# The last tile's closing layer norm and residual: a shorter merge, the inverse root on GpSimd, and scale and residual fused on VectorE

## The reference

```python
x = x + LN(attention(LN(x)))     # 16 heads of 8, projections with bias
x = x + LN(ffn(LN(x)))           # 32 experts, top 6 of 4 of 8 groups, squared relu, and a shared expert
```

## Time and profile before

| | |
|---|---|
| three runs | 541.24 us median (538.66, 541.24, 541.57) |
| the profiled execution | 542.95 us, of which 540.9 us are the span from the first to the last instruction |
| granted TensorE clock | 0.98 on average |
| busy | PE 90%, DVE 74%, ACT 66%, POOL 32% of the span |
| last matmul group of the feed-forward part | ends at about 531.0 us of the span |
| last tile's closing norm, from the copy at 530.99 to the end | 9.9 us |

### The profile page before, as it was taken

One profiled execution on the slowest core, in us unless ns is written; L12 is line 12 of the kernel. 1 busy time (PEld: TensorE's weight loads), 2 busy tenths in 40 slices (PEclk: granted clock), 3 DMA queues, 4 the chain that ended last, 5 costly groups with the idle time before them and its releaser, 6 DMA issues.

```text
span 540.9 us, 10853 instructions
## 1 busy us (share of the span) xinstructions
PE 484.6 (90%) x3376; PEld 270.5 (50%) x3376; DVE 398.8 (74%) x1072; ACT 359.0 (66%) x708; POOL 170.8 (32%) x500
## 2 busy tenths in 40 slices
PE   2457997989999999998899999999999999999993
PEld 1212443444444444444345665666656665666661
DVE  4678786879999989898725859587776859485453
ACT  2424786758888988888685566757756666755442
POOL 5054231323544435320002223515152533302020
PEclk9999999989999999999699999999999999999998
DMA  6334356333333333331014343535263544535321
GB/s 186 108 118 144 97 173 195 122 117 116 106 110 98 114 109 115 115 114 38 3 60 141 117 162 118 193 103 196 87 179 115 180 157 138 196 100 197 138 78 39
DMA packets 52456, 67.47 MB, mean 125 GB/s; under 512 B 5168, under 2 KB 36784, under 8 KB 52144
## 3 DMA queue, kind: packets, MB, share of 16 engines
q1 hardware_dynamic: 52400, 66.78, 39.2%
HBM read 51.17 MB, written 15.20 MB: 123 GB/s over the span
## 4 chain that ended last, share of the span: by engine, by line
PE 70%; DVE 7%; ACT 7%; SPq 5%; issue 5%; POOL 3%; DMA 2%; ACTq 0%; POOLq 0%; DVEq 0%
PE pY L1278 12%; PE pS L1278 12%; PE pO L1199 8%; PE pS L1264 6%; PE pS L1266 6%; PE pS L1265 6%; PE pS L1143 6%; PE pS L1149 3%; DVE mneg L859 3%; ACT probs L643 2%; SPq L387 2%; SPq L375 2%; PE pX L1128 2%; DMA k_scratch<-k_parts 2%; PE pX L1131 1%
## 5 line engine op out<-in xcount | busy, mean ns | idle before, releaser
L859 DVE TENSOR_REDUCE mneg<-pS 128x2 f32<-128x512 f32 x256 | 164.2, 686 | 31.8 <-PE pS L1143 31.0
L643 ACT ACTIVATE probs<-pS 128x512 f32<-128x512 f32 x256 | 143.9, 595 | 31.7 <-PE pS L1149 30.3
L718 ACT ACTIVATE h_ring<-r 128x512 f32<-128x512 f32 x144 | 90.4, 629 | 88.9 <-DVE r L1013 68.3
L1013 DVE SCALAR_TENSOR_TENSOR r<-pS,c_ring 128x512 f32<-128x512 f32 x128 | 87.6, 689 | 45.6 <-PE pS L1266 44.2
L1143 PE MATMUL pS<-kp,qp 48*128 48x256 bf16 x512 | 88.8, 295 | 24.9 <-DVE mneg L859 9.9
L1264 PE MATMUL pS<-qp,up_hi 128*128 128x512 f32 x144 | 103.5, 719 | 0.0
L1149 PE MATMUL pS<-qp,kp 51*128 51x256 bf16 x512 | 89.1, 287 | 0.8 <-ACT probs L643 0.5
L1199 PE MATMUL pO<-probs,vv 128*32 128x256 f32 x1024 | 76.6, 408 | 0.4 <-ACT oT_sb L594 0.4
L1278 PE MATMUL pS<-h_ring,down_sb 128*128 128x512 f32 x144 | 73.8, 594 | 0.0
L1278 PE MATMUL pY<-h_ring,down_sb 128*128 128x512 f32 x144 | 73.4, 595 | 0.0
L1143 PEld LDWEIGHTS pS<-kp,qp 48*128 48x128 bf16 x512 | 34.9, 97 | 75.3 <-DVE mneg L859 41.7
(11 more groups left out here) (178 smaller groups left out, 682.3 us busy)
## 6 DMA issues: line engine op xcount, KB each, us to landing
c_ring<-c_scratch SPq DMA_DIRECT2D x64, 512.0 KB, 3.9
qp<-q_scratch SPq DMA_DIRECT2D x64, 96.0 KB
kp<-k_scratch SPq DMA_DIRECT2D x64, 96.0 KB
q_scratch<-q_parts SPq DMA_DIRECT2D x16, 192.0 KB, 2.3
k_scratch<-k_parts SPq DMA_DIRECT2D x16, 192.0 KB, 2.4
q_scratch<-q_parts SPq DMA_DIRECT2D x16, 128.0 KB, 2.2
k_scratch<-k_parts SPq DMA_DIRECT2D x16, 128.0 KB, 2.2
out_x<-ot SPq DMA_DIRECT2D x7, 256.0 KB, 4.5
```

Source lines behind the costliest of these rows:

```text
L643: nc.scalar.activation(probs[j][:, hh], pS2[n % S2_RING][:, :, :], ACT.Exp, scale=SCALE).then_inc(exp_done, 1)
L718: nc.scalar.activation(h_sb[n % HRING], r_sb[n % URING][:, :], ACT.Square).then_inc(sq_done, 1)
L859: nc.vector.tensor_reduce(mneg[u % 2][:, :, hh, k], pS1[n % S1_RING][:, :].rearrange("p (a s) -> p a s", a=TH), AX.X, ALU.max, negate=True ...
L1013: nc.vector.scalar_tensor_tensor(out=r_sb[n % URING][:, :], in0=pU[n % URING], scalar=0.0, in1=c_ring[group % CRING][:, at], op0=ALU.max, ...
```

## The change

Only the closing norm of tile 7 is changed.

- **Merge.** 0.25·d·d is now one instruction (`scalar_tensor_tensor`) in place of two (L324 and L327), and the −0.5·m of L325 is no longer an instruction. The order is d, m, v, then v/128 + eps, 0.25·d·d, v + that.
- **Root.** DVE signals `var4_done` after the variance. POOL, at the end of its stream, waits for it and writes `rs4` = variance to the power −0.5, then signals `root4_done`. The Newton rounds, `half` and `nm4` of this tile are gone.
- **Mean.** DVE subtracts the mean from all four pieces in one instruction, `fn` = −0.5·m + `pN`, 128 × 512, with m (128 × 4) broadcast.
- **Scale and residual.** DVE does `ot` = `fn`·rs4 + `xbig` in one instruction of 128 × 128 for each of the four pieces, with `rs4` as a scalar for each partition. Every second one raises `ot_last`. ACT's four `norm_f` pieces of this tile, and DVE's two adds, are gone.
- SP's two stores and their waits are the same.

```diff
@@ gpsimd, after the loop over the tiles
+            pool.wait_ge(var4_done, 1)
+            nc.gpsimd.tensor_tensor(rs4[:, :], work4[0][:, :], power[:, 0:C4], ALU.pow).then_inc(root4_done, 1)
@@ scalar, norm_f
-                if i == NTILE - 1:
-                    ins.then_inc(fn_last, 1)
-                elif c == C4 - 1:
+                if c == C4 - 1:
                     ins.then_inc(fn_done, 1)
@@ scalar, the end
             keep_fT(NTILE - 1)
-            for c in range(C4):
-                norm_f(NTILE - 1, c)
@@ vector, the end
             stats_f(NTILE - 1)
             dve.wait_ge(f_stats, NTILE)
-            norm_chain(nc.vector, dve.wait_ge, Link(dve, ln4_last, 0), stats4[:, :, :], [w[:, :] for w in work4],
-                       rs4[:, :], nm4[:, :], (fn_done, NTILE - 1), fused=True).then_inc(ln4_done, 1)
-            for half in range(2):
-                dve.wait_ge(fn_last, C4 // 2 * (half + 1))
-                if half == 0:
-                    dve.wait_ge(stored[(NTILE - 1) % 2], 16 * (NTILE // 2 - 1))
-                cs = slice(C4 // 2 * half, C4 // 2 * (half + 1))
-                nc.vector.tensor_tensor(ot[(NTILE - 1) % 2][:, cs], fn[:, cs],
-                                        xbig[:, NT - C4 + cs.start:NT - C4 + cs.stop], ALU.add).then_inc(ot_last, 1)
+            v, t, m, d, half = [w[:, :] for w in work4]
+            even, odd = stats4[:, :, 0:3], stats4[:, :, 3:6]
+            link = Link(dve, ln4_last, 0)
+            nc.vector.tensor_tensor(d, even[:, :, 1], odd[:, :, 1], ALU.subtract)
+            nc.vector.tensor_tensor(m, even[:, :, 1], odd[:, :, 1], ALU.add)
+            link(nc.vector.tensor_tensor(v, even[:, :, 2], odd[:, :, 2], ALU.add))
+            nc.vector.tensor_scalar(v, v, 1.0 / D, EPS, ALU.mult, ALU.add)
+            link(nc.vector.scalar_tensor_tensor(out=d, in0=d, scalar=0.25, in1=d, op0=ALU.mult, op1=ALU.mult))
+            nc.vector.tensor_tensor(v, v, d, ALU.add).then_inc(var4_done, 1)
+
+            dve.wait_ge(fn_done, NTILE - 1)
+            dve.wait_ge(ot_done, NTILE - 1)
+            link(nc.vector.scalar_tensor_tensor(out=fn[:, :, :], in0=m.unsqueeze(2).to_broadcast((P, C4, D)), scalar=-0.5,
+                                                in1=pN[:, :].rearrange("p (c d) -> p c d", c=C4),
+                                                op0=ALU.mult, op1=ALU.add))
+            dve.wait_ge(stored[(NTILE - 1) % 2], 16 * (NTILE // 2 - 1))
+            dve.wait_ge(root4_done, 1)
+            for c in range(C4):
+                ins = nc.vector.scalar_tensor_tensor(out=ot[(NTILE - 1) % 2][:, c], in0=fn[:, c], scalar=rs4[:, c:c + 1],
+                                                     in1=xbig[:, NT - C4 + c], op0=ALU.mult, op1=ALU.add)
+                if c % 2:
+                    ins.then_inc(ot_last, 1)
```

More of the change, by code:

```diff
@@ L291, in block_kernel @@
         fn_done = sem("fn_done")
-        fn_last = sem("fn_last")
+        var4_done, root4_done = sem("var4_done"), sem("root4_done")
         ln4_last = sem("ln4_last")
```

## The result

Over 13 runs the changed kernel has a median of 538.91 us (536.74 to 541.86), the kernel before, in 13 runs (three of them those known before the prediction), 542.5 (538.66 to 544.81). The ratio is 0.9949, with a 95% interval of 0.9928 to 0.9970: faster, by 0.3% to 0.7%. The two medians by themselves lie 3.6 us apart, 0.66%, which this interval also holds. The forecast was 539.0 and 2.2 us, 0.41%, within it too. The median of the ratio lies just past the 0.5% that I had called the limit of what can be told; its interval holds both sides of it.

The account below looks back on a forecast made before the run. Matmuls bound the whole span, a serial chain the tail. Merge 0.27, root by POOL 1.12 and last pass 0.85 make 2.24; 2.2 off the median 541.24 gives 539.0 us, range 536.5 to 540.3.

Parts of the forecast that it names:

- Merge: Tile 7's closing statistics: variance ready at 534.05 in place of 534.32, 0.27 us saved by the new order.
- Power: Root on POOL: starts 0.08 behind DVE's variance and takes 1.04, from 534.13 to 535.17.
- Subtraction: DVE's mean subtraction: 0.69, broadcast at no cost, hidden under the power with 0.55 to spare.
- Back to DVE: Hand-over from POOL's power to DVE's first piece: 0.04, so DVE goes on at 535.21.
- Pieces: Four scale-and-residual instructions on DVE: steps of 0.26, duration 0.34, 1.12 in all; bounds 0.89 and 1.36.
- Stores: SP's two issues at L462: 0.52 apart, before 0.69; 2.3 from the second issue to the end.
- Sum: Whole tail: second store begins at 536.35 in place of 538.58, 2.23 us saved.
- shared read path: Rival: the subtraction holds up POOL's power, all behind it 0.53 later, gain 1.7, 539.5; chance 0.07.
- The power was not long: Rival, slower than before: a power of 3.3 us takes all the gain, 4.20 ends at 542.2; chance 0.02.
- Tile 6's store: Rival, no effect: this store, landing at about 532.4, ends the span if it takes 6 us more; chance 0.01.
- A measured ratio past 0.5%: Rival: the gain shows as over 0.5%, with cheaper pieces and power 2.5 us, 0.46%, 538.7; chance 0.2.
- A sign that was wrong: Stated sign: the prediction is wrong if the time before 533 us has moved, which nothing in the change explains.

Follow-up runs that it names:

- e4: Changed kernel with the root made by Newton rounds on DVE again, ahead of the subtraction; merge start to last issue 4.76 us, against 3.19.
- e3: Changed kernel with the subtraction reading `fT_sb` (SBUF) in place of `pN` (PSUM); power 1.40 in place of 1.02, merge start to last issue 3.585 us.
- e1: Changed kernel with the root's wait written first of the three ahead of the first piece; merge start to last issue 3.08 us, against 3.19.
- e2: Changed kernel with pieces multiplying by constant 1.0 in place of rs4; pieces 0.90 in place of 1.14, merge start to last issue 2.96 us.
- e5: Changed kernel with the last pass undone (nm4, four ACT pieces, two adds), short merge and POOL's root kept; merge start to last issue 4.10 us.
- e10: e2 with the second store issued from ACT's queue; merge start to last issue 2.94 us, to the end of the span 5.28.
- e9: e8 with three stores (pieces 0 and 1 SP, 2 ACT, 3 SP); tail 5.14 us, median 539.98, ratio 0.9959 to the kernel before.
- e6: Changed kernel with the power in two instructions of 2 columns and the root's wait first; merge start to last issue 2.905 us.
- e8: Changed kernel with powers of 3 and 1 columns, subtraction written into PSUM, root's wait first; merge start to last issue 2.905 us, tail 5.22.

## Why the prediction was right

- **Merge.** Forecast v + d ending 0.79 behind the merge's start, measured 531.50 − 530.72 = 0.78. The fused 0.25·d·d takes 0.16, as its neighbours.
- **Power.** DVE to POOL 0.08, as forecast; 1.02, where 1.04 was taken (the value of L529 in rows 4, not of L333 in rows 3).
- **Subtraction.** 0.69, under the power, over 0.49 before it ends: 531.42 + 0.69 = 532.11 against 532.60. Its broadcast costs nothing: 0.69 as in L1013. e4 shows what the cover is worth, 0.72, and e3 what it would cost to read both tensors from SBUF, 0.4. The forecast speaks of seven linked DVE steps that the power replaces; nine Newton instructions follow each other by links (e4 has them again, in 2.04). The sum did not use the count.
- **Back to DVE.** The one term that was off: 0.14 in place of 0.04. I had taken the 0.04 from a piece with one late wait, and passed over that the new piece has three waits ahead of it, and that the late one was written last. Everything else was within 0.02. e1 gives the 0.10 back by their order alone.
- **Pieces.** Forecast 1.12, measured 1.14. e2 confirms the split, a step of 0.20 and 0.06 for the scalar. Rows 7, from which the 0.06 came, compare instructions that also differ in where they read and in the type they write, so that it came out exactly is partly luck. The pieces do overlap. The rule quoted from the Trainium skill (VectorE: DVE Perf Modes, The DRAIN you can't avoid), by which they would take 1.36, was quoted without the exception that the section makes, that a next operation which is not held starts earlier. The steps of 0.20 and 0.26 agree with the exception.
- **Stores.** Two issues 0.525 apart, forecast 0.52, 1.8 to landing, and 2.3 from the last to the end. What I had not seen is how little more there was to gain by bringing them nearer: at 0.42 apart the second issue is 0.47 long, and of 0.23 only 0.13 reach the end (e2).
- **Sum.** Forecast 2.23, measured 2.13 (to the last issue) or 2.16 (to the end). e1 has 5.32 − 3.08 = 2.24. Two of the three parts were undone one at a time, root 1.57 (e4) and last pass 0.91 (e5); the third, the merge, is read from the rows as 0.28 (variance ready at 1.06 before, 0.78 after). They add up to 2.76, more than the 2.13, because the subtraction's 0.72 is counted in the root's part: in e4 the fused pass costs it, and in e5 it isn't there. The 0.09 that is then missing is the wait of 0.10, which neither e4 nor e5 has, so that it is taken off twice.
- **Rivals.** The shared read path did not take part, for the reason given (one tensor in PSUM); e3 puts its price at 0.4 and not 0.53. The power was not long. Tile 6's store, taken to land in the 1.8 of the last two, took 2.3 before; it was still over 5 us from setting the end. A measured ratio past 0.5% did come out, at 0.9949. The tail says 2.16/542.5 = 0.40%, so the rest fits the noise between executions.
- **The absolute time.** That 539.0 was forecast and 538.91 measured is luck. The forecast was taken down from a median of three runs, 541.24. Over 13 runs the kernel before has 542.5, and 2.2 less than that is 540.3, the upper end of the stated range. What was right is the length of the tail.
- **A sign that was wrong.** The prediction was to be wrong if the time before 533 us had moved. It moved, by 2.54, and this says nothing against the mechanism: it moves by as much from one execution to the next of the same kernel. The sign was set without a look at that.

## What to carry to other kernels

At the end of a kernel, where one instruction waits for the next, sum start-to-start steps and hand-overs from rows of the same shape; here each term was forecast to 0.02 but one, and a gain of 2.13 to 0.1, though runs vary by 3 us. Judge it by a stretch of the trace that begins where the streams first differ, not by the spans of two profiles. When several waits stand ahead of an instruction on the critical path, write the one that ends last first, so that the instruction itself carries it. And where a merged row gives the start of the first instruction and the length of both, look at the second alone before a theory is built on its start.

## What the runs showed of the hardware that I had not expected

- The first piece begins 0.14 behind the end of the power when the root's wait stands in DVE's queue by itself (0.03 to the wait, 0.05 of its own, 0.06 to the piece), and 0.04 behind it when the piece carries the wait (e1).
- The second of SP's two issues of 128 KB stores took 0.47 when it began 0.42 behind the first (e2), and 0.37 to 0.38 when it began 0.52 to 0.70 behind it (all others with two). ACT's took 0.42 at 0.41 behind SP's (e10); one of 64 KB took 0.37 at 0.26 behind (e9).
- A store of 64 KB took the same 1.8 to landing as one of 128 KB in one execution (e9).
- DVE with two SBUF tensors holds POOL's power up by 0.38 when it starts first (e3), but a power of 2 columns that starts first does not hold DVE (e6). The Trainium skill (SBUF — State Buffer, Who interferes with whom) says that a Vector instruction with two SBUF inputs contends with a GpSimd one that reads SBUF. e3 agrees, with 1.40 in place of 1.02; e6 does not, with 0.70 and 1.29 against 0.70 and 1.28.
- GpSimd's power costs about 0.39 and 0.16 for each column of 128 rows (e6, e8).
